# Distance lanes of a DTW kernel: one trip through memory in two parts, distances on unsplit fp32

## The chip, the cores and the metric

The kernel runs on one core of a Trainium2 chip. The metric is the device time of one execution, in microseconds (us). The engines are TensorE (PE), VectorE (DVE), ScalarE (ACT), GpSimd (POOL) and SyncE (SP, which only issues DMAs here).

## The reference

Two blocks, each a cross attention with a gate and a feed forward with a gate. The change touches only the "attention" of the first block, which is dynamic time warping of the 77 context rows against the 512 normalised tokens of each of 4 batches:

```
D = sqrt(max(aa + bb - 2 a @ b.T, 0))          # a: ctx 77x128, b: layernorm(x) 512x128
R[i,j] = D[i,j] + min(R[i-1,j], R[i,j-1], R[i-1,j-1])
path  = backtrack R from (76, 511) to (0, 0)   # first of diagonal, up, left that is smallest
x     = x + tanh(g_xattn[0]) * (sum over path of ctx[i] into row j)
x     = x + tanh(g_ffn[0])   * MoE(layernorm(x), 64 experts of 64, top 8, a shared expert)
x     = x + tanh(g_xattn[1]) * attention(layernorm(x), ctx, 16 heads)
x     = x + tanh(g_ffn[1])   * MoE(layernorm(x), 8 experts of 344, top 2, a shared expert)
```

## The kernel before

Each engine has one instruction stream, written out by hand; semaphores join them, and nothing reorders. The stages before the first feed forward are these.

**Norm.** `norm(0)` goes over the four batches b. DVE takes statistics and normalises three of four 128x128 tiles (`normalise`, L1244), GpSimd the fourth (L601). TensorE transposes them into a PSUM bank (`turn`, L951). ScalarE copies the bank to `xn_hi` in fp32r (`high`, L741) and squares it into `sq` (L744), and DVE forms the rest, `xn_lo` (`low`, L1253). `context` prepares the context: -2 times its transpose split into `ctxT_hi` (ACT, L728) and `ctxT_lo` (DVE, L1326), and its squared sums `aa` (L1329).

**Distances.** `distances(b)` on TensorE adds four products into a bank: hi by hi (L967), lo by hi (L968), ones by `sq` (L970, fp32) and hi by `xn_lo` (L972). ScalarE then does, for one batch after another, Relu with bias `aa` (L776), Sqrt (L778) and Square of the root (L780). The root is corrected in `corrected(b)` on DVE: an integer estimate of 1/(2 root) (L1340), the error d2 - root^2 (GpSimd at L642 for batches 0 to 2, DVE at L1345 for batch 3), times the estimate (L1347), plus the root (L1349).

**Lanes.** The recurrence runs as a skewed wave: 16 lanes for each batch (partitions 32b to 32b+15), 32 columns for each lane, 92 slots in time. The corrected rows (77 partitions) must become lanes with a skew, and go through memory for it: SP stores `drows` of each batch into `scr_d`, which was zeroed from the cleared lane buffer `dl` (GpSimd memset, L583), with a destination step that gives the skew (L463, 154 KB in runs of 128 bytes), and loads it back as lanes (L467, 184 KB, 16 rows of 11.8 KB). All four stores are issued ahead of the first load. DVE, SP and GpSimd wait for all four loads.

**Wave and path.** DVE runs 92 slots of four or five small instructions (L1384 to L1388, L1376), then 92 slots back (L1423 to L1427). The path goes through memory in three parts (`store_path` L406, `load_path` L413), half of the batches on SP's queue, half on ACT's; TensorE multiplies it with the context (L1006), and `norm(1)` begins. Beside the wave, GpSimd, TensorE and ScalarE transpose the weights of the second feed forward (`prep_in`, L632, L995, L806).

Before the wave, DVE also clears the edges of the backward pass (L1356 to L1360) and splits the first two groups of weights (`first_lo(0)`, L1366); the latter lets SP load the next group (`raw0(2, 0)`).

Of the kernel before, what the change touches and what calls it, by code (L numbers as in the profile page):

```python
# [29 lines left out]
P = 128  # L30
# [5 lines left out]
def program(nc, x, ctx_1024, g_xattn, g_ffn, r0_w, sg0, su0, sd0, eg0, eu0, ed0,  # L36
# [12 lines left out]
    SLOTS = KEYS + CH - 1  # L49
    LANE = SLOTS * CW  # L50
# [48 lines left out]
    with ctx:  # L99
# [31 lines left out]
        gates = sb("gates", [P, 4])  # L131
        tgate = sb("tgate", [P, 4])
        ctx_sb = sb("ctx_sb", [KEYS, B, H])
        ctxT = sb("ctxT", [P, B, KEYS])
        ctxT_hi = sb("ctxT_hi", [P, B, KEYS], F32R)
        ctxT_lo = sb("ctxT_lo", [P, B, KEYS], F32R)
# [58 lines left out]
        drows = view([B, S])  # L195
# [138 lines left out]
        s_cthi = sem("ctxT_hi_ready")  # L334
        s_ctlo = sem("ctxT_lo_ready")
# [4 lines left out]
        s_err = sem("dist_root_error")  # L340
        s_dist = sem("dist_ready")
        s_dst = [sem(f"dist_stored{b}") for b in range(B)]
        s_dld = [sem(f"dist_lanes{b}") for b in range(B)]
# [22 lines left out]
        def wait_low(engine, k, b):  # L366

            pool_before = POOL_LOW * min(max(k - 1, 0), 2)
            if k in (1, 2) and b < POOL_LOW:
                engine.wait_ge(s_xlp, pool_before + b + 1)  # L370
            else:
                engine.wait_ge(s_xlo, B * k + b + 1 - pool_before - (POOL_LOW if k in (1, 2) else 0))
# [28 lines left out]

        def store_path(engine, part, b):
# [14 lines left out]
        POOL_CONST = 10 + B  # L417
# [3 lines left out]
        def _(sp):  # L421
# [34 lines left out]
            sp.wait_ge(s_pool, POOL_CONST)  # L456
# [3 lines left out]
            for b in range(B):  # L460

                sp.wait_ge(s_dist, b + 1)
                sp.dma_start(at(scr_d[b], 0, [[CW, KEYS], [LANE + CW, CH], [1, CW]]),  # L463
                             drows[0:KEYS, b, :].rearrange("i (c w) -> i c w", w=CW)).then_inc(s_dst[b], 16)
            for b in range(B):
                sp.wait_ge(s_dst[b], 16)
                sp.dma_start(dl[LANES[b]:LANES[b] + CH].rearrange("c s w -> c (s w)"),  # L467
                             scr_d[b].rearrange("c s w -> c (s w)")).then_inc(s_dld[b], 16)

            for b in range(B):  # L470
                sp.wait_ge(s_dld[b], 16)
# [9 lines left out]
            sp.wait_ge(FF[0]["wlo"], 1)  # L481
            raw0(2, 0)
            for part in range(len(ON_PARTS)):
                for b in range(B // 2):
                    store_path(sp, part, b)
                for b in range(B // 2):
                    load_path(sp, part, b)

# [78 lines left out]
        def _(pool):  # L567
# [15 lines left out]
            nc.gpsimd.memset(dl, 0.0).then_inc(s_pool, 1)  # L583
            nc.gpsimd.memset(rst[:, 0, :], BIG).then_inc(s_pool, 1)
            pool.wait_ge(s_pool, 10)
# [37 lines left out]
            for g in range(GROUPS[1]):  # L623
# [14 lines left out]
                if g == 1:  # L638
                    for b in range(B - 1):

                        pool.wait_ge(s_root, b + 1)
                        nc.gpsimd.tensor_tensor(d2[0:KEYS, b, :], d2[0:KEYS, b, :], droot2[0:KEYS, b, :],  # L642
                                                ALU.subtract).then_inc(s_err, 1)
                    attention_prep()
                    for b in range(B):
                        pool.wait_ge(s_dld[b], 16)
# [77 lines left out]
        def _(act):  # L724
            def context():
                act.wait_ge(s_ct, 1)
                nc.scalar.activation(ctxT[:], ps[6][:, 0:B * KEYS].rearrange("p (b k) -> p b k", b=B), ACT.Copy)
                nc.scalar.activation(ctxT_hi[:], ps[6][:, 0:B * KEYS].rearrange("p (b k) -> p b k", b=B),  # L728
                                     ACT.Copy, scale=-2.0).then_inc(s_cthi, 1)
# [7 lines left out]
            def high(k, b):  # L737
                act.wait_ge(s_xt, B * k + b + 1)
                bank = turn_bank(k, b)
                if k == 0:  # L740
                    nc.scalar.activation(xn_hi[:, sl(b)], bank[:], ACT.Copy).then_inc(s_xhi, 1)  # L741
# [3 lines left out]
                else:  # L745
# [3 lines left out]
                    nc.scalar.activation(xn_hi[:, sl(b)], bank[:], ACT.Copy).then_inc(s_xhi, 1)  # L749

# [6 lines left out]
            def norm(k):  # L757
                for b in range(B):
# [5 lines left out]
                    if k == 2 and b >= 2:  # L764
                        query(b - 2)
                if k in (0, 2):
# [4 lines left out]

            norm(0)
            act.wait_ge(s_aa, 1)
            for b in range(B):
                act.wait_ge(s_ab, b + 1)
                nc.scalar.activation(d2[0:KEYS, b, :], dist_bank(b), ACT.Relu, bias=aa[:, b:b + 1]).then_inc(s_d2, 1)  # L776
                act.wait_ge(s_d2, b + 1)
# [934 lines left out]
```

## Time and profile before

| | us |
|---|---|
| median of three timed runs | 823.42 (819.32 to 824.99) |
| the profiled execution's own time | 818.27 |
| its span | 816.3 |
| busy in the span: TensorE, VectorE, ScalarE, GpSimd | 666.1, 624.9, 412.2, 412.8 |

The profiled execution is one run; about 2 us of its time lie around the span. The busy shares are averages over stages: from 44 to 160 us VectorE works alone through the wave, and from 200 us on TensorE is almost always busy.

### The profile page before, as it was taken

To read this page: it belongs to the slowest core of one execution; us is meant where nothing else is said; L and a number is where in the kernel's file an instruction comes from. 1 tells how busy PE (TensorE), PEld (TensorE's weight loads), DVE (VectorE), ACT (ScalarE), POOL (GpSimd) and SP (SyncE) were. 2 spreads that over 40 slices of the span, in tenths; PEclk is the share of its full clock that TensorE was granted. 3 is DMA by queue.
4 is the path that set the end of the run, shared out by engine and by line. 5 is a ranking of instruction groups with operands and counts; after the bars stand their busy time and mean duration, and the time that the engine had idled before them with its cause. 6 is when DMAs were issued, how large, how long until landed. Compare 5 with 4: busy or idle time off the path is not lost.

```text
span 816.3 us, 13236 instructions
## 1 busy us (share of the span) xinstructions
PE 666.1 (82%) x3082; PEld 535.1 (66%) x3082; DVE 624.9 (77%) x2076; ACT 412.2 (50%) x755; POOL 412.8 (51%) x448
## 2 busy tenths in 40 slices
PE   4412320089999999999999969999899999999995
PEld 2201110077787887888888748999878888888884
DVE  7689999877777777777777688777777777777774
ACT  3524410044566566656656555555556656665663
POOL 5367750026666666666666641110146666666663
PEclk9655555558999999999999969999789999999999
DMA  5545331104967676777767300000126666566761
GB/s 136 81 108 144 117 108 33 32 5 94 169 143 161 136 156 135 161 144 151 155 136 161 80 0 12 1 0 0 37 39 138 160 147 153 132 165 137 154 141 52
DMA packets 78728, 85.97 MB, mean 105 GB/s; under 512 B 44085, under 2 KB 56742, under 8 KB 75620
## 3 DMA queue, kind: packets, MB, share of 16 engines
q1 hardware_dynamic: 71638, 75.23, 43.6%
q0 software_dynamic: 4320, 9.68, 4.0%
q10 hardware_dynamic: 2734, 0.69, 0.4%
q8 instruction: 10, 0.16, 0.1%
q14 instruction: 26, 0.21, 0.1%
HBM read 76.69 MB, written 8.70 MB: 105 GB/s over the span
## 4 chain that ended last, share of the span: by engine, by line
PE 70%; DVE 20%; issue 4%; DMA 2%; ACT 2%; POOL 1%; DVEq 0%; ACTq 0%; POOLq 0%
PE bank L1012 14%; PE bank L1014 14%; PE bank L1013 14%; PE bank L1147 7%; PE bank L1145 6%; PE bank L1144 6%; PE bank L1074 4%; DVE arena L1427 3%; PE bank L1058 2%; DVE arena L1423 2%; DVE arena L1384 2%; DVE arena L1376 2%; DVE arena L1424 1%; DVE arena L1385 1%; PE bank L951 1%
## 5 line engine op out<-in xcount | busy, mean ns | idle before, releaser
L701 POOL TENSOR_TENSOR act_lo<-arena,act_hi 128x512 fp32r<-128x512 f32 x232 | 300.3, 1294 | 194.6 <-ACT act_hi L841 152.8
L1644 DVE TENSOR_TENSOR bank<-arena,bank 128x512 f32<-128x512 f32 x220 | 152.4, 693 | 102.9 <-ACT arena L855 71.8
L855 ACT ACTIVATE arena<-bank 128x512 f32<-128x512 f32 x232 | 139.2, 600 | 180.6 <-PE bank L1014 180.6
L1012 PE MATMUL bank<-xn_hi,w_hi 128*128 128x512 f32 x464 | 186.5, 402 | 1.2 <-DVE arena L1642 1.2
L1014 PE MATMUL bank<-xn_lo,w_hi 128*128 128x512 f32 x464 | 184.8, 398 | 0.0
L1013 PE MATMUL bank<-xn_hi,w_lo 128*128 128x512 f32 x464 | 184.2, 397 | 0.0
L1652 DVE TENSOR_TENSOR arena<-bank,arena 128x512 f32<-128x512 f32 x220 | 152.1, 691 | 13.8 <-DMA arena<-scr_mask 1.6
L841 ACT ACTIVATE act_hi<-arena 128x512 fp32r<-128x512 f32 x232 | 145.4, 627 | 9.3 <-DVE arena L1642 5.9
L1012 PEld LDWEIGHTS bank<-xn_hi,w_hi 128*128 128x128 f32 x464 | 88.4, 190 | 24.4 <-issue 2.0
L1014 PEld LDWEIGHTS bank<-xn_lo,w_hi 128*128 128x128 f32 x464 | 88.3, 190 | 21.9
L1013 PEld LDWEIGHTS bank<-xn_hi,w_lo 128*128 128x128 f32 x464 | 88.4, 190 | 21.0
L1147 PE MATMUL bank<-act_lo,w_hi 128*128 128x512 f32 x232 | 92.7, 399 | 3.3 <-POOL act_lo L701 3.3
L1145 PE MATMUL bank<-act_hi,w_lo 128*128 128x512 f32 x232 | 92.1, 397 | 0.0
L1144 PE MATMUL bank<-act_hi,w_hi 128*128 128x512 f32 x232 | 91.3, 393 | 0.0
L995 PE MATMUL bank<-ident,prep_in 128*128 128x128 f32 x75 | 22.5, 438 | 62.1 <-DMA prep_in<-in_L_ffn_wd 60.3
L601 POOL TENSOR_SCALAR xn<-x_res,mv,rstd 128x128 f32<-128x128 f32 x16 | 14.1, 883 | 96.7 <-DVE rstd L1301 72.6
L995 PEld LDWEIGHTS bank<-ident,prep_in 128*128 128x128 f32 x75 | 12.6, 213 | 72.0 <-DMA prep_in<-in_L_ffn_wd 70.2
L1147 PEld LDWEIGHTS bank<-act_lo,w_hi 128*128 128x128 f32 x232 | 43.6, 188 | 15.3 <-POOL act_lo L701 5.9
L1628 DVE TENSOR_TENSOR w_lo<-w_raw,w_hi 128x384 fp32r<-128x384 f32 x54 | 50.9, 943 | 0.8 <-ACT w_hi L849 0.8
L1144 PEld LDWEIGHTS bank<-act_hi,w_hi 128*128 128x128 f32 x232 | 43.6, 188 | 10.6 <-ACT act_hi L841 0.5
L1145 PEld LDWEIGHTS bank<-act_hi,w_lo 128*128 128x128 f32 x232 | 43.6, 188 | 10.1
L1006 PE MATMUL bank<-ctx_sb,arena 77*128 77x128 f32 x32 | 7.2, 425 | 47.4 <-DMA arena<-scr_on 47.4
(188 smaller groups left out, 949.2 us busy)
## 6 DMA issues: line engine op xcount, KB each, us to landing
arena<-scr_mask SPq DMA_DIRECT2D x94, 512.0 KB, 6.6
scr_w<-prep_out POOLq DMA_DIRECT2D x25, 192.0 KB, 2.2
w_raw<-scr_w SPq DMA_DIRECT2D x25, 192.0 KB, 6.3
w_raw<-in_L_ffn_expert_gate_k SPq DMA_DIRECT2D x32, 64.0 KB, 6.0
w_raw<-in_L_ffn_expert_up_k SPq DMA_DIRECT2D x32, 64.0 KB, 5.7
w_raw<-in_L_ffn_expert_down_k SPq DMA_DIRECT2D x64, 32.0 KB, 5.3
prep_in<-in_L_ffn_wg POOLq DMA_DIRECT2D x21, 64.0 KB, 2.4
prep_in<-in_L_ffn_wu POOLq DMA_DIRECT2D x21, 64.0 KB, 2.1
```

The source lines that it names most:

```text
L701: nc.gpsimd.tensor_tensor(act_lo[:, k % 2, :], act_a[:, k % 2, :], act_hi[:, k % 2, :].bitcast(F32), ALU.subtract).then_inc(FF[f]["alo"], 1)
L841: nc.scalar.activation(act_hi[:, j, :], act_a[:, j, :], ACT.Copy).then_inc(FF[f]["ahi"], 1)
L855: nc.scalar.activation(act_s[:, k % 2, :], ps[4 + k % 2][:], ACT.Silu).then_inc(FF[f]["silu"], 1)
L1012: nc.tensor.matmul(out, w_h, x_h, start=start, stop=False)
L1013: nc.tensor.matmul(out, w_l, x_h, start=False, stop=False)
L1014: return nc.tensor.matmul(out, w_h, x_l, start=False, stop=stop)
L1144: nc.tensor.matmul(ps[n][:], w_hi[:, j, DOWN:DOWN + P], act_hi[:, i, :], start=first, stop=False)
L1145: nc.tensor.matmul(ps[n][:], w_lo[:, j, DOWN:DOWN + P], act_hi[:, i, :], start=False, stop=False)
L1147: nc.tensor.matmul(ps[n][:], w_hi[:, j, DOWN:DOWN + P], act_lo[:, i, :], start=False, stop=last).then_inc(FF[f]["down"], 1)
L1628: nc.vector.tensor_tensor(w_lo[:, j, :], w_raw[:, j, :], w_hi[:, j, :].bitcast(F32), ALU.subtract).then_inc(FF[f]["wlo"], 1)
L1644: nc.vector.tensor_tensor(ps[6 + i][:], act_s[:, i, :], ps[6 + i][:], ALU.mult).then_inc(FF[f]["t"], 1)
L1652: nc.vector.tensor_tensor(act_a[:, i, :], ps[6 + i][:], mask[:, j, 512 * k:512 * (k + 1)], ALU.mult).then_inc(FF[f]["act"], 1)
```

## The change

1. The distances are formed on fp32 operands as they are: `xT0` (ScalarE's copy of the transposed tokens) times `ctxT_neg`, plus ones by `sq`. `ctxT_lo`, `xn_lo` of norm 0 and their waits are gone. `xT0` takes the place of `drows` in the arena, and `corrected` writes its result into `d2`.
2. DVE forms the root's error for all four batches; GpSimd's three instructions are gone.
3. ScalarE clears `dl` at the very start (L583's memset is gone from GpSimd), after a Sqrt of one column that has the table loaded; it does `dist_root(0)` ahead of `high(0, 3)`.
4. Each batch is stored in two parts (rows 0 to 23 and 24 to 76), and loaded in two (slots 0 to 23 and 24 to 91). The first part's loads are issued among the stores. DVE waits for the first parts ahead of slot 0 and for the second ahead of slot 24. SP and GpSimd wait for the first parts only.
5. The edges of the backward pass are cleared inside the wave (slots 16 to 21), and `first_lo(0)` follows the last path cells; SP's `raw0(2, 0)` follows the path's DMAs.

```diff
+    LSPLIT = 24
+    DIST_PARTS = [(0, LSPLIT), (LSPLIT, KEYS)]
+    LANE_PARTS = [(0, LSPLIT), (LSPLIT, SLOTS)]
...
+        def store_dist(engine, part, b):
+            first, last = DIST_PARTS[part]
+            engine.dma_start(at(scr_d[b], first * CW, [[CW, last - first], [LANE + CW, CH], [1, CW]]),
+                             d2[first:last, b, :].rearrange("i (c w) -> i c w", w=CW)).then_inc(s_dst[part][b], 16)
+        def load_lanes(engine, part, b):
+            first, last = LANE_PARTS[part]
+            for p in range(part + 1):
+                engine.wait_ge(s_dst[p][b], 16)
+            engine.dma_start(dl[LANES[b]:LANES[b] + CH, first:last].rearrange("c s w -> c (s w)"),
+                             scr_d[b, :, first:last].rearrange("c s w -> c (s w)")).then_inc(s_dld[part][b], 16)
+        def lanes_laid(engine, part):
+            for b in range(B):
+                engine.wait_ge(s_dld[part][b], 16)
...
             for b in range(B):
                 sp.wait_ge(s_dist, b + 1)
-                sp.dma_start(at(scr_d[b], 0, ...), drows[0:KEYS, b, :]...).then_inc(s_dst[b], 16)
+                store_dist(sp, 0, b)
+                store_dist(sp, 1, b)
+                if b >= 1:
+                    load_lanes(sp, 0, b - 1)
+            load_lanes(sp, 0, B - 1)
             for b in range(B):
-                sp.wait_ge(s_dst[b], 16)
-                sp.dma_start(dl[LANES[b]:LANES[b] + CH]..., scr_d[b]...).then_inc(s_dld[b], 16)
-            for b in range(B):
-                sp.wait_ge(s_dld[b], 16)
+                load_lanes(sp, 1, b)
+            lanes_laid(sp, 0)
...
-            nc.gpsimd.memset(dl, 0.0).then_inc(s_pool, 1)
...
+            nc.scalar.activation(root_one[:], ones[:, 0:1], ACT.Sqrt)
+            nc.scalar.activation(dl, ones[:, 0:CW].unsqueeze(1).broadcast_to([P, SLOTS, CW]), ACT.Copy, scale=0.0).then_inc(s_blank, 1)
             norm(0)
-            for b in range(B):
+            for b in range(1, B):
+                dist_root(b)
...
+                if k == 0:
+                    act.wait_ge(s_aa, 1)
+                    dist_root(0)
                 if k in (0, 2):
                     high(k, B - 1)
...
-                nc.tensor.matmul(d, ctxT_hi[:, b, :], xn_hi[:, sl(b)], start=True, stop=False)
-                nc.tensor.matmul(d, ctxT_lo[:, b, :], xn_hi[:, sl(b)], start=False, stop=False)
+                nc.tensor.matmul(dist_bank(b), ctxT_neg[:, b, :], xT0[:, b, :], start=True, stop=False)
                 pe.wait_ge(s_sq, b + 1)
-                nc.tensor.matmul(d, ones[:, 0:KEYS], sq[:, b % 2, :], start=False, stop=False)
-                pe.wait_ge(s_xlo, b + 1)
-                nc.tensor.matmul(d, ctxT_hi[:, b, :], xn_lo[:, sl(b)], start=False, stop=True).then_inc(s_ab, 1)
+                nc.tensor.matmul(dist_bank(b), ones[:, 0:KEYS], sq[:, b % 2, :], start=False, stop=True).then_inc(s_ab, 1)
...
-                if b < B - 1:
-                    dve.wait_ge(s_err, b + 1)
-                else:
-                    inv = done(nc.vector.tensor_tensor(d2[0:KEYS, b, :], d2[0:KEYS, b, :], droot2[0:KEYS, b, :], ALU.subtract))
+                inv = done(nc.vector.tensor_tensor(d2[0:KEYS, b, :], d2[0:KEYS, b, :], droot2[0:KEYS, b, :], ALU.subtract))
...
-            first_lo(0)
-            for b in range(B):
-                dve.wait_ge(s_dld[b], 16)
...
+                if s in (0, LSPLIT):
+                    lanes_laid(dve, 0 if s == 0 else 1)
...
+                if CH <= s < CH + 2 + B:
+                    back_edge(s - CH)
...
             cells(SLOTS // PIECE - 1)
+            first_lo(0)
```

Three places in the instruction streams show it. The names in brackets are semaphores: `dist_ready` counts corrected batches, `dist_stored` and `dist_lanes` the landings of stores and loads.

ScalarE, end of the norm and first roots, before:

```order
L741 ACTIVATE xn_hi<-bank 128x512 [waits xn_transposed]
L744 ACTIVATE arena<-bank 128x512 [waits dist_products]
L741 ACTIVATE xn_hi<-bank 128x512 [waits xn_transposed]
L744 ACTIVATE arena<-bank 128x512 [waits dist_products]
L776 ACTIVATE arena<-bank,aa 77x512 [waits dist_products,ctx_squared_sums]
L778 ACTIVATE arena<-arena 77x512 [waits dist_squared]
L780 ACTIVATE arena<-arena 77x512 [waits act_step]
```

and the same place after the change:

```order
L753 ACTIVATE arena<-bank 128x512 [waits xn_transposed]
L756 ACTIVATE arena<-bank 128x512 [waits dist_products]
L766 ACTIVATE arena<-bank,aa 77x512 [waits dist_products,ctx_squared_sums]
L768 ACTIVATE arena<-arena 77x512 [waits dist_squared]
L770 ACTIVATE arena<-arena 77x512 [waits act_step]
L753 ACTIVATE arena<-bank 128x512 [waits xn_transposed]
L756 ACTIVATE arena<-bank 128x512 [waits dist_products]
```

The three steps of `dist_root(0)` now stand ahead of the copy and the square of batch 3.

SP's queue, from the zeroing of the scratch to the first copy of the values, before:

```order
L457 DMA scr_d<-arena 64x2944 [waits pool_step]
L463 DMA scr_d<-arena 77x16x32 [waits dist_ready,scratch_zeroed]
L463 DMA scr_d<-arena 77x16x32 [waits dist_ready] x3
L467 DMA arena<-scr_d 16x2944 [waits dist_stored0]
L467 DMA arena<-scr_d 16x2944 [waits dist_stored1]
L467 DMA arena<-scr_d 16x2944 [waits dist_stored2]
L467 DMA arena<-scr_d 16x2944 [waits dist_stored3]
L478 DMA v_flat<-v_ext 77x4x9 [waits dist_lanes3,dist_lanes2,v_ready,dist_lanes1,dist_lanes0]
```

and after the change, from batch 2 on:

```order
L407 DMA scr_d<-arena 24x16x32 [waits dist_ready]
L407 DMA scr_d<-arena 53x16x32
L415 DMA arena<-scr_d 16x768 [waits dist_stored0_1]
L407 DMA scr_d<-arena 24x16x32 [waits dist_ready]
L407 DMA scr_d<-arena 53x16x32
L415 DMA arena<-scr_d 16x768 [waits dist_stored0_2]
L415 DMA arena<-scr_d 16x768 [waits dist_stored0_3]
L415 DMA arena<-scr_d 16x2176 [waits dist_stored1_0,dist_stored0_0]
L415 DMA arena<-scr_d 16x2176 [waits dist_stored1_1,dist_stored0_1]
L415 DMA arena<-scr_d 16x2176 [waits dist_stored1_2,dist_stored0_2]
L415 DMA arena<-scr_d 16x2176 [waits dist_stored1_3,dist_stored0_3]
L497 DMA v_flat<-v_ext 77x4x9 [waits dist_lanes0_3,dist_lanes0_2,v_ready,dist_lanes0_1,dist_lanes0_0]
```

The load of each first part stands behind the next batch's stores, and the large loads stand behind all of them.

VectorE, from the last batch's correction to the wave's first slot, before:

```order
L1340 TENSOR_SCALAR arena<-arena 77x512 [waits dist_root]
L1345 TENSOR_TENSOR arena<-arena 77x512
L1347 TENSOR_TENSOR arena<-arena 77x512 [waits dve_step]
L1349 TENSOR_TENSOR arena<-arena 77x512 [waits dve_step]
L1356 MEMSET arena 128x32 [waits dist_ready,pool_step]
L1357 MEMSET arena 128x33
L1360 MEMSET arena 16x33 [waits dve_step]
L1360 MEMSET arena 16x33 x3
L1366 TENSOR_TENSOR w_lo<-w_raw,w_hi 128x384 [waits ff0_whi,dve_step]
L1366 TENSOR_TENSOR w_lo<-w_raw,w_hi 128x384 [waits ff0_whi]
L1384 STREAM_SHUFFLE arena<-arena 128x1 [waits dist_lanes2,dist_lanes3,dist_lanes1,dist_lanes0]
```

and after the change:

```order
L1349 TENSOR_SCALAR arena<-arena 77x512 [waits dist_root]
L1351 TENSOR_TENSOR arena<-arena 77x512
L1353 TENSOR_TENSOR arena<-arena 77x512 [waits dve_step]
L1355 TENSOR_TENSOR arena<-arena 77x512 [waits dve_step]
L1392 STREAM_SHUFFLE arena<-arena 128x1 [waits dist_lanes0_2,dist_lanes0_1,dist_lanes0_3,dist_lanes0_0,pool_step]
```

Nothing stands between the correction and the wave any more; each of the four batches now has the four instructions that only batch 3 had.

## Rows read from the trace of the kernel before

**Rows 1.** Chain that ended last, first 200 us: start us, us, what.

```profile
16.77 0.57 PE bank L951 x4
...
34.53 3.00 DMA scr_d<-arena
37.55 6.10 DMA arena<-scr_d
...
162.19 2.62 DMA arena<-scr_on
```

**Rows 2.** Timeline of VectorE: start us, us, engine, line, operation; idle before in brackets.

```profile
43.78 0.01 DVE L1384 LOAD_MASK_SELECT arena<-arena  x1 [7.34 <-DMA arena<-scr_d]
...
46.26 0.15 DVE L1384 STREAM_SHUFFLE arena<-arena 128x1 f32<-128x1 f32 x1
```

**Rows 3.** Timeline of the start: GpSimd's clearing, and VectorE.

```profile
3.64 2.55 POOL L583 MEMSET arena<- 128x2944 f32 x1
...
6.62 0.18 DVE L1279 RECIPROCAL rstd<-std 128x4 f32<-128x4 f32 x1 [0.35 <-ACT std L735]
```

**Rows 4.** Loads of x issued from 1.7 to 2.2 us (one, at 1.84).

```profile
DMA to landing us min/median/max: 4.6/4.6/4.6
```

**Rows 5.** ScalarE's instructions by line and form: busy us, mean ns.

```profile
L890 ACT ACTIVATE arena<-arena 128x1232 f32<-128x1232 f32 x16 | 19.7, 1232 | 9.8 <-DVE arena L1539 9.8
```

**Rows 6.** Chain, first 22 us: TensorE's products of batch 0 and of batch 1.

```profile
12.43 1.35 PE bank L951 x4
...
14.63 1.71 PE bank L970 x2
...
17.33 0.23 PE bank L967
...
17.79 0.86 PE bank L970 x2
```

**Rows 7.** Timeline of ScalarE: end of the norm, first roots, last context step.

```profile
19.36 0.60 ACT L741 ACTIVATE xn_hi<-bank 128x512 fp32r<-128x512 f32 x1 [0.90 <-PE bank L951]
...
20.33 0.68 ACT L776 ACTIVATE arena<-bank,aa 77x512 f32<-77x512 f32 x1
...
22.24 0.67 ACT L776 ACTIVATE arena<-bank,aa 77x512 f32<-77x512 f32 x1
...
30.04 0.51 ACT L789 ACTIVATE kT_hi<-bank,bias 128x308 fp32r<-128x308 f32 x1
```

**Rows 8.** Timeline of VectorE and GpSimd while the roots are corrected.

```profile
22.44 1.52 DVE L1340 TENSOR_SCALAR arena<-arena 77x512 int32<-77x512 int32 x1 [1.27 <-ACT arena L780]
...
29.28 0.42 DVE L1340 TENSOR_SCALAR arena<-arena 77x512 int32<-77x512 int32 x1
...
29.80 0.69 DVE L1347 TENSOR_TENSOR arena<-arena 77x512 f32<-77x512 f32 x1
...
30.52 0.69 DVE L1349 TENSOR_TENSOR arena<-arena 77x512 f32<-77x512 f32 x1
30.63 0.89 POOL L594 TENSOR_TENSOR wq_lo<-w,wq_hi 128x128 fp32r<-128x128 f32 x1 [3.07 <-ACT kT_hi L789]
...
31.49 1.03 POOL L595 TENSOR_TENSOR kT_lo<-kT,kT_hi 128x308 fp32r<-128x308 f32 x1
...
31.73 1.33 DVE L1345 TENSOR_TENSOR arena<-arena 77x512 f32<-77x512 f32 x1
```

**Rows 9.** Issue to landing of the first lane load, at 34.86 us.

```profile
DMA to landing us min/median/max: 4.5/4.5/4.5
```

**Rows 10.** Issue to landing of the path's last stores (24 KB each, from 160.68 us).

```profile
DMA to landing us min/median/max: 1.5/1.6/1.7
```

**Rows 11.** Timeline of VectorE after the correction.

```profile
34.84 0.53 DVE L1360 MEMSET arena<- 16x33 f32 x4
35.41 1.03 DVE L1366 TENSOR_TENSOR w_lo<-w_raw,w_hi 128x384 fp32r<-128x384 f32 x2
```

**Rows 12.** Windows: busy us of PE, PEld, DVE, ACT, POOL; granted clock; DMA share; GB/s.

```profile
580.00:600.00 20.00, 18.50 (x72) 16.01 (x72) 16.50 (x95) 9.77 (x19) 3.88 (x4) 0.57 0.15 37
```

More of the change, by code:

```diff
@@ L339, in program @@
         s_root = sem("dist_root")
-        s_err = sem("dist_root_error")
         s_dist = sem("dist_ready")
-        s_dst = [sem(f"dist_stored{b}") for b in range(B)]
-        s_dld = [sem(f"dist_lanes{b}") for b in range(B)]
+        s_blank = sem("lanes_blank")
+        s_dst = [[sem(f"dist_stored{part}_{b}") for b in range(B)] for part in range(2)]
+        s_dld = [[sem(f"dist_lanes{part}_{b}") for b in range(B)] for part in range(2)]
         s_upper = sem("wave_upper")
@@ L371, in wait_low @@
             else:
-                engine.wait_ge(s_xlo, B * k + b + 1 - pool_before - (POOL_LOW if k in (1, 2) else 0))
+                engine.wait_ge(s_xlo, B * (k - 1) + b + 1 - pool_before - (POOL_LOW if k in (1, 2) else 0))
         def query_bank(n):
@@ L487, in _ @@
                     load_path(sp, part, b)
+            sp.wait_ge(FF[0]["wlo"], 1)
+            raw0(2, 0)
             def mask0(g, j, chunks, loaded):
@@ L638, in _ @@
                 if g == 1:
[L639 to L643, printed above, removed]
                     attention_prep()
-                    for b in range(B):
-                        pool.wait_ge(s_dld[b], 16)
+                    lanes_laid(pool, 0)
                 if g >= 1:
@@ L1309, in norm @@
                         context()
-                    if k == 0 and p >= 1:
-                        low(k, p - 1)
                     if k in (1, 2) and p > POOL_LOW:
@@ L1315, in norm @@
                         query(p - 2)
-                low(k, B - 1)
+                if k > 0:
+                    low(k, B - 1)
                 if k == 2:
@@ L1367, in first_lo, with back_edge @@
                                             ALU.subtract).then_inc(FF[f]["wlo"], 1)
-            first_lo(0)
-            for b in range(B):
-                dve.wait_ge(s_dld[b], 16)
+            def back_edge(step):
+                if step == 0:
+                    done(nc.vector.memset(lg[:, SLOTS, :, :], 0.0))
+                if step == 1:
+                    done(nc.vector.memset(qex[:, SLOTS, :], 0.0))
+                    settle()
+                if step >= 2:
+                    b = step - 2
+                    done(nc.vector.memset(qex[LANES[b]:LANES[b] + CH, SLOTS, :], 1.0))
             shift = [31] + list(range(CH - 1)) + [31] * (32 - CH)
```

68 lines of the change are left out of this document (24 added, 44 removed).

## The prediction

> **What bounds the kernel now.** I read the chain that ended last first. Up to 200 us it is one thread: norm, TensorE's products, ScalarE's roots, VectorE's correction, then two DMAs in a row, then the wave. The two DMAs are 3.00 us of store and 6.10 us of load, of batch 3 [rows 1], and the timeline of VectorE shows the same from its side: it sits idle for 7.34 us until the last lanes land, and the wave starts at 43.78 [rows 2]. So what counts is when the wave starts and whether the wave, the path and the feed forwards behind it keep their length. Nothing else in the first 44 us is worth anything by itself. The sum is made against the profiled execution's 818.27 us.
>
> **Before the distances.** GpSimd's clearing of `dl` takes 2.55 us and ends at 6.19; VectorE's next stage begins at 6.62 [rows 3]. It also needs batch 1 of x, which lands at 1.84 + 4.6 = 6.44 [rows 4], so freeing GpSimd gives 0.15 us at most here. ScalarE's clearing is 2944 columns; a form of 1232 columns takes 1.23 us [rows 5], so I put it at some 2.9 us, behind a table load that it has anyway. It ends near 5.2, when ScalarE's first work of the norm isn't ready. Cost 0. Dropping `ctxT_lo` takes some 0.25 us off VectorE, `xn_lo` of batch 0 another 0.6; so TensorE's second set of transposes, at 12.43 now [rows 6], starts at 12.0 and ends at 13.4.
>
> **TensorE.** Of the four products, ones by `sq` is fp32 and takes 1.71 us for batch 0 and 0.86 us for batch 1; an fp32r product takes 0.23 us at that later rate [rows 6]. The engine runs at half rate until about 16.7 us and at full rate after it. The new pair is twice fp32: 1.72 us in place of 0.86 + 3 x 0.23 = 1.55 at the full rate, and 3.4 in place of 3.0 at the half rate. Batch 0 is therefore done at 13.4 + 3.4 = 16.8, a little less if the rate rises as early as it starts work, and the transposes of batch 2 start where they start now, at 16.77 [rows 1]. The earlier start is spent on the longer product: gain 0.
>
> **ScalarE.** The transposes of batch 2 are done at 17.35. One copy and square take 20.33 - 19.36 = 0.97 us [rows 7], so `dist_root(0)` can start at 18.4, its product being done at 16.8. From there to VectorE's start is 22.44 - 20.33 = 2.11 us [rows 7, 8]: 20.5 in place of 22.44. The next batches of roots follow 1.91 us apart [rows 7], but batch 3's copy and square stand in between: `dist_root(1)` starts at 18.4 + 1.91 + 0.97 = 21.3, and roots 1, 2, 3 are there for VectorE at 23.4, 25.3 and 27.2.
>
> **VectorE's correction.** In peace L1340 takes 0.42, and two products in a row start 0.72 apart [rows 8]. One batch is then 0.4 + 0.72 + 0.72 + 0.61 = 2.45 us. Batch 0 runs 20.5 to 22.9, batch 1 23.4 to 25.9, batch 2 to 28.3, batch 3 to 30.8. Now it ends at 34.53 [rows 1], since GpSimd's share costs more than it takes off: L1340 took 1.52 us beside GpSimd's subtraction in place of 0.42, and L1345 1.33 beside `kT_lo` [rows 8]. One such meeting stays. ScalarE's last context step ends at 30.55, which is 4.5 us behind the start of `dist_root(3)` (20.33 + 3 x 1.91 = 26.06) [rows 7]; after the change that is 25.1 + 4.5 = 29.6, in the middle of batch 3, and `wq_lo` (0.89) and `kT_lo` (1.03) [rows 8] follow it. Bounds 0 and 1.9 us; I take 0.5, since VectorE's L1349 was not held up by `wq_lo` and its turn came between the two. Done at 31.3: **3.2 us earlier** (bounds 1.7 and 3.7).
>
> The Trainium skill (SBUF — State Buffer, "Who interferes with whom") says that a VectorE instruction with two SBUF inputs contends with a GpSimd one that reads SBUF, and that the first to issue keeps the other out for its whole length. The rows agree (L1345 31.73 to 33.06, GpSimd until 32.52) [rows 8]. By it the loss is that of whoever comes first, 0.5 or 1.5 us, within my bounds.
>
> **The two DMAs.** Before, 34.53 to 43.78: 9.25 us. The load's 6.10 are not its own: the first of the four loads took 4.5 us [rows 9], and the last one queued behind three. A part of 24 rows is 48 KB. For its store the nearest rows are 1.5 to 1.7 us (24 KB, long runs) [rows 10] and 3.00 (154 KB in runs of 128 bytes) [rows 1]; I take 2.1, since a third of the runs lies nearer to the small one. For its load, 3 KB a row, they are 2.62 for the path's last loads [rows 1], four at once on two queues, and 4.5 for rows of 11.8 KB [rows 9]; alone it should be less than 2.62, and I take 2.1, with 1.6 as the low end. With 0.1 for the semaphores that makes 4.3: **4.95 us less** (bounds 2.8 and 5.9). The loads of batches 0 to 2 are hidden in the correction; batch 3's second store, issued 0.3 us after the first, is moving its data while the first part's load is still being prepared.
>
> Here a rule speaks against the change. The Trainium skill (DMA: Bandwidth & Descriptors, "Anatomy of one DMA") puts a DMA at about 2.0 us plus its bytes over 436 GB/s, so that halves cost almost what the whole does. For the new pair it gives 4.2 us, like my sum; for the old pair it would give 4.8, where the rows have 9.1 [rows 1]. Here the measurement decides. By the rule's difference alone, 0.6 us in place of 4.95, the sum at the end would be 3.2 us.
>
> The wave starts at 31.3 + 4.3 = **35.6 in place of 43.78**, 8.2 us earlier.
>
> **The wave and behind it.** A slot is 0.61 us (four from 43.81 to 46.26) [rows 2]; slot 24 comes 14.7 us after the start, at 50.3. The four second loads are issued by about 35.5, and four larger ones landed 9 us after the first was issued (34.86 to 43.78); even with the values' copies and GpSimd's weights on the same queues they have 5 us in hand: cost 0. The six clearings of the edge move from a wait into the wave. Four took 0.53 us [rows 11], so six are 0.8 in full; a slot has gaps of 0.16, so 0.25 is the low end; I take **0.6 added**. `first_lo(0)`, 1.03 us [rows 11], moves to where VectorE waits for the path's last trip, until beyond 164.8 from 160.7 [rows 1]; cost 0, or 1 if its cover were gone. It releases `raw0(2, 0)`, four issues on SP that stand behind the path's loads and whose group is used some 40 us later. GpSimd's preparation of weights waits for first parts now and moves with the wave.
>
> **Sum.** 3.2 + 4.95 = 8.2 (rounded) less 0.6 = **7.6 us**: 818.27 becomes 810.7. The profiled execution lies 5.15 us below the median of the timed runs, 823.42, so I forecast 823.4 - 7.6 = **815.8**. The bounds of the terms give 1.7 + 2.8 - 0.8 = 3.7 to 3.7 + 5.9 - 0.25 = 9.4, or 814.0 to 819.7.
>
> **Rivals.**
> 1. TensorE stays at the half rate through all distances. For: it has the rate of batch 0 [rows 6], and more work. Against: it rose at 16.7 us with the engine at work since 12.43, and after the change the engine works at least as densely, without the wait for `xn_lo`. Each batch then takes 3.4 + 1.35 us, the last product ends at 29.8, the correction 2.1 + 2.5 later at 34.4; the gain is 0.1 + 4.95 - 0.6 = 4.5: 818.9.
> 2. The legs don't shrink with the size. If the part's load takes the 4.5 us of [rows 9] and its store 3.0 [rows 1], the two give 9.25 - 7.6 = 1.65 and the sum is 4.3: 819.1. The rule of the Trainium skill named above (DMA: Bandwidth & Descriptors) says the same more strongly; with its difference alone one would be at 820.2.
> 3. The other side: the granted clock. Between 580 and 600 us it averaged 0.57 [rows 12], a stretch at 1.2 GHz that covers most of the window while TensorE is 92% busy, and no cause in the kernel is visible. Were such a stretch longer after the shift, each microsecond of full-rate work in it would cost one more; from 7.6 us of work on the change is a loss, and with 20 us it would be 12 us slower: 828. Against it: the work behind the wave is the same, in the same order.
> 4. The change does more than I take: the store and load at their low ends and no meeting with GpSimd, a gain of 9.4: 814.0.
>
> **How the numbers follow.** About 1% (8.2 us) is what a measurement of this kernel can tell from no change, since its own runs differ by 0.7%. The forecast's case (gain 5.5 to 8.6) gets 0.55, rival 4 0.2, rival 1 0.06, rival 2 0.12, rival 3 0.04, the rest 0.03. The timed runs before scatter by -4 and +1.6 us round their median. With that, 0.35 of the forecast's case and 0.9 of rival 4 end beyond 1%, and a fifth of rivals 1 and 2: 0.19 + 0.18 + 0.04, and 0.01 of the rest, is 0.42 for faster by over 1%. Slower by over 1% is rival 3 and 0.01 of the rest, 0.05; within 1% is what is left, 0.53. The range runs from 823.4 - 9.4 and the runs' scatter, 809, to rival 2 and a little scatter, 821.
>
> **What would show it.** The wave's first slot at 35.6 (34.4 to 40); the idle time ahead of it near 4.3 us; the first correction starting at 20.5 and the last one done at 31.3; the loads of first parts landing in some 2.1 us; no wait at slot 24; the wave's span longer by 0.6; the path's last trip and the feed forwards unchanged. It would be wrong if batch 3's first part landed late behind other traffic, if the wave were slowed by GpSimd's earlier work, or if a stretch of low clock moved.

## The result, and the profile after

| | before | changed |
|---|---|---|
| median of timed runs, us | 821.37 (818.05 to 824.99, 4 runs) | 846.03 (844.62 to 847.24, 4 runs) |
| ratio | | 1.0294 [1.0261, 1.0327] |
| span of the profiled execution, us | 816.3 | 844.5 |

The change costs 24.7 us; the prediction had it gain 7.6. The range (809 to 821) doesn't hold the result, and the rival on the slower side isn't what happened either.

The chain that ended last, of the changed kernel, answers to [rows 1] (columns: start, us, what):

```profile
16.22 0.45 PE bank L972 x4
...
29.11 0.85 DVE arena L1355
29.95 2.16 SPq L407
32.16 0.36 SPq L407
32.56 9.88 SPq L415
42.48 0.38 SPq L407
42.90 0.32 SPq L407
43.27 9.57 SPq L415
52.88 0.38 SPq L407
53.31 0.32 SPq L407
53.67 9.49 SPq L415
63.20 2.84 DMA arena<-scr_d
...
183.91 1.49 DMA scr_on<-arena
185.41 2.33 DMA arena<-scr_on
```

Up to 29.95 the thread is the old one, and it is early: before, the last correction ended at 34.53. Then comes what the chain of before doesn't have at all: 33 us of `SPq`, the issuing of DMAs on SP. Three issues of a load of a first part (L415) last 9.5 to 9.9 us each, where two stores in a row (L407) take 0.7. The timeline of VectorE shows the other side, against [rows 2]:

```profile
66.17 0.01 DVE L1392 LOAD_MASK_SELECT arena<-arena  x1 [36.23 <-DMA arena<-scr_d]
```

The idle time ahead of the wave grew from 7.34 us to 36.23, and the wave starts at 66.17 in place of 43.78, 22.4 us later.

What the DMAs do in that time is in the DMA view of 22 to 60 us (40 slices of 0.95 us: busy tenths of the 16 DMA engines, and GB/s), and in a window (us, busy time of PE, PEld, DVE, ACT, POOL, then granted clock, DMA share, GB/s):

```profile
DMA  0300111111140111111111510111111116111111
GB/s 0 55 14 13 11 11 11 11 11 11 11 58 11 11 11 11 11 11 11 11 11 11 99 21 11 11 11 11 11 11 11 11 11 106 15 11 11 11 11 11
```

```profile
34.00:41.00 7.00, 0.00 (x0) 0.00 (x0) 0.00 (x0) 0.00 (x0) 0.00 (x0) 0.50 0.10 11
```

The peaks are the first parts, 24 rows each. All the rest is a flat 11 GB/s: 106 KB of a second store at 11 GB/s are 9.6 us, which is the length of the long issues. A single store of 77 rows moved ten times as fast, as one more window of the kernel before shows (its first store, of batch 0, under way):

```profile
27.40:28.60 1.20, 1.20 (x5) 0.63 (x4) 1.10 (x2) 1.18 (x2) 0.16 (x1) 0.50 0.82 128
```

So the store of rows 24 to 76, in the same runs of 128 bytes, moves at a twelfth of the rate of the store of rows 0 to 76. The two differ in the number of rows: 77 = 7 x 11, and 53 is a prime. The Trainium skill (DMA: Bandwidth & Descriptors, "Why a DMA increments its semaphore by 16 and not by 1") says that a DMA runs on the largest number of engines up to 16 that divides the slowest dimension of both its sides, and on HWDGE (the way of DMAs that SP issues) on the lowest-numbered ones. By it 77 rows run on 11 engines, 24 on 12, and 53 on one. The measured rates agree with it: 128/11 = 11.6 GB/s for each engine, and 11 for one. So does a count in the traces. There the last packets of a DMA are completions of 4 bytes, which raise its semaphore. The DMA view of 27.2 to 28.8 us of the kernel before holds one store of 77 rows, which is 77 x 16 = 1232 runs of 128 bytes and 11 packets more:

```profile
DMA packets 1243, 0.16 MB, mean 99 GB/s; under 512 B 1243, under 2 KB 1243, under 8 KB 1243
```

The updates of each store's semaphore give the same count, after one early update at the issue: 11 at 77 rows and at 22 and 55, 12 at 24, 10 at 20, 9 at 54, 3 at 57, and 1 at 53 and at 23. In all kernels here it is the largest divisor up to 16. Which engines they are the traces don't say. The experiments change the number of rows and look at what becomes of the time.

Of the rest, rows that answer to [rows 3, 7, 8]:

```profile
2.21 2.64 ACT L798 ACTIVATE arena<-ones 128x2944 f32<-128x2944 f32 x1
6.30 0.18 DVE L1292 RECIPROCAL rstd<-std 128x4 f32<-128x4 f32 x1 [0.85 <-DMA x_res<-in_x]
19.77 0.42 DVE L1349 TENSOR_SCALAR arena<-arena 77x512 int32<-77x512 int32 x1 [3.33 <-ACT arena L770]
22.57 0.42 DVE L1349 TENSOR_SCALAR arena<-arena 77x512 int32<-77x512 int32 x1 [0.33 <-ACT arena L770]
28.94 0.45 POOL L612 TENSOR_TENSOR wq_lo<-w,wq_hi 128x128 fp32r<-128x128 f32 x1 [9.18 <-ACT kT_hi L810]
29.11 0.84 DVE L1355 TENSOR_TENSOR arena<-arena 77x512 f32<-77x512 f32 x1
```

The estimate L1349 takes 0.42 us each time, where L1340 had taken 1.52 in its place. From the wave's start on little is new: from its start to the last path cell 117.74 us (66.17 to 183.91) against 116.90, and no wait at slot 24. From the last path cell to the end of the span this execution has 660.6 us and the profiled one of before 655.6. That isn't the change: the profiled executions of e1 to e12 lie between 657.4 and 662.6, e6's, which has before's code behind the wave, at 660.0. Before's is the short one, beside e10's. The granted clock there is low in stretches, as in [rows 12]; here in three windows of the changed kernel:

```profile
600.00:610.00 10.00, 8.88 (x42) 8.44 (x41) 5.01 (x21) 3.26 (x10) 1.74 (x2) 0.50 0.00 0
610.00:620.00 10.00, 9.31 (x44) 8.62 (x43) 7.26 (x28) 4.92 (x9) 1.73 (x2) 0.50 0.32 75
620.00:630.00 10.00, 9.35 (x31) 6.50 (x32) 9.43 (x65) 4.95 (x8) 2.60 (x2) 0.84 0.00 0
```

The stretch at 1.2 GHz is longer here: 23.9 us by the clock's own records, against 17.1 in the profiled execution of before. The experiments have 23.9 or 27.4, but for e10's 17.1, so the short stretch goes with the short executions and not with the kernel before as such. What sets its length no run shows. With the two terms of the wave, 22.4 + 0.84 = 23.2 us stand beside the 24.7 of the medians.

### The profile page after: what moved, and what is told of

Same layout as the page of the kernel before. It is cut to its first block, busy times and chain, and to the rows that moved or that the text cites. A ratio compares the mean times of both kernels' runs of the same rounds, so it can differ in the third digit from the quotient of the medians.

```text
span 844.5 us, 13234 instructions
## 1 busy us (share of the span) xinstructions
PE 671.7 (80%) x3078; PEld 537.6 (64%) x3078; DVE 619.4 (73%) x2074; ACT 415.1 (49%) x757; POOL 406.7 (48%) x444
## 4 chain that ended last, share of the span: by engine, by line
PE 69%; DVE 18%; SPq 4%; issue 3%; ACT 2%; DMA 1%; POOL 1%; DVEq 0%; ACTq 0%; POOLq 0%
PE bank L1029 14%; PE bank L1031 14%; PE bank L1030 14%; PE bank L1164 6%; PE bank L1161 6%; PE bank L1162 6%; PE bank L1091 4%; SPq L415 3%; DVE arena L1438 3%; PE bank L1075 2%; DVE arena L1434 2%; DVE arena L1392 2%; DVE arena L1382 1%; DVE arena L1435 1%; DVE arena L1393 1%
## 5 line engine op out<-in xcount | busy, mean ns | idle before, releaser
L1029 PEld LDWEIGHTS bank<-xn_hi,w_hi 128*128 128x128 f32 x464 | 88.1, 190 | 24.7 <-DVE arena L1654 2.2
L827 ACT ACTIVATE prep_out<-bank 128x384 f32<-128x384 f32 x25 | 12.3, 490 | 82.1 <-PE bank L1012 82.1
```

Of the source, the lines that this page charges most:

```text
L1029: nc.tensor.matmul(out, w_h, x_h, start=start, stop=False)
```

## Experiments

Each is one edit of the changed kernel unless it says otherwise. Where the timed kernel has a ratio, it is to the kernel before, run beside it. Theory A is the number of rows; theory B the order and number of the DMAs on SP's queue, whatever their rows, theory C that a second store of this size in short runs is too much ahead of the loads, whatever its rows. Theory D, in e5 and e6, is about the rest of the change: in e5 that it costs time as well, in e6 that it gains none.

**e1: 22 and 55 rows**

```diff
-    LSPLIT = 24
+    LSPLIT = 22
```

> The changed kernel with the parts cut at row and slot 22 instead of 24, so the stores have 22 and 55 rows. Theory A (a store is spread over as many DMA engines as the largest number up to 16 that divides its row count; 53 is prime, so the second store ran on one engine at 11 GB/s, 9.5 us each, and held SP's queue): 22 and 55 both divide by 11, as 77 does, so the stores take some 1.2 us of data each, SP's issues are short, the wave starts at 34 to 35 instead of 66.15, and the kernel takes 812 to 816. Theory B (stores and loads alternating on one queue, or 16 DMAs instead of 8, hold SP's queue): nothing changes, 846. Theory C (the second store's 106 KB in runs of 128 bytes is simply too much ahead of the loads): with 55 rows it is a little worse, 847.

Measured: 815.35 (811.56 to 815.87), ratio 0.9901 [0.9865, 0.9938]. Two rows fewer in the first part take 30.7 us away. The chain, and the timeline of SP and VectorE:

```profile
30.73 1.67 DMA scr_d<-arena
32.42 1.91 DMA arena<-scr_d
```

```profile
26.61 0.56 SPq L415 DMA_DIRECT2D arena<-scr_d  x1
28.20 0.74 SPq L407 DMA_DIRECT2D scr_d<-arena  x2
28.98 0.54 SPq L415 DMA_DIRECT2D arena<-scr_d  x1
...
34.46 0.01 DVE L1392 LOAD_MASK_SELECT arena<-arena  x1 [3.76 <-DMA arena<-scr_d]
```

The load's issue is 0.55 us and the wave starts at 34.46. A window of 24 to 25 us has the stores' rate:

```profile
24.00:25.00 1.00, 0.00 (x0) 0.00 (x0) 0.96 (x2) 0.97 (x2) 0.00 (x0) 1.00 0.70 106
```

Same two parts, same order, same queue: the order and the split as such are not the cause.

**e2: 24 rows and 53, but the 53 as 48 and 5**

```diff
+            for r0, r1 in ([(first, last)] if part == 0 else [(first, first + 48), (first + 48, last)]):
```

> The changed kernel with the second store of each batch issued as two, of 48 and 5 rows; same bytes, one DMA more for each batch. Theory A: 48 rows go on 16 engines and 5 rows on 5, so the wave starts at about 35 and the time is some 813 to 817. Theory B: one more DMA in the same queue, at least as slow as the change, 846 or more. Theory C: as slow, 846.

One run: 814.81 (before beside it 823.11). The wave starts at 33.13:

```profile
33.13 0.01 DVE L1393 LOAD_MASK_SELECT arena<-arena  x1 [3.87 <-DMA arena<-scr_d]
```

The cut is that of the changed kernel and there is one DMA more in each batch, so neither the cut at 24 nor the number of DMAs costs anything. What was slow was the one DMA of 53 rows.

**e3: 23 and 54 rows**

```diff
-    LSPLIT = 24
+    LSPLIT = 23
```

> The changed kernel cut at 23, so the stores have 23 and 54 rows. Theory A: 23 is prime, so the first store, 47 KB, runs on one engine: 4.1 us of data, while the 54 rows go on 9 engines. The wave waits for the first part, so it starts about 3 us later than with 22 and 55: 37 to 39, and 816 to 820; SP's issues of the next DMA are held for up to 4 us. Theory B and C: as the change, 846, since one row more or less makes no difference.

One run: 827.03 (before beside it 823.11). Now the first part is the prime one. Windows of 23 to 26 us, and of 27.5 to 28 with a store of 54 rows:

```profile
23.00:26.00 3.00, 0.28 (x1) 0.30 (x2) 2.79 (x6) 2.91 (x6) 0.00 (x0) 1.00 0.07 10
```

```profile
27.50:28.00 0.50, 0.50 (x4) 0.33 (x2) 0.50 (x2) 0.50 (x1) 0.00 (x0) 0.50 0.72 107
```

10 GB/s for 23 rows and 107 for 54: the slow part moves with the prime. The place was right and the size was not, in the time (816 to 820 expected) as in the wave, which started at 46.85 and not at 37 to 39. I had counted batch 3's store alone, and four slow stores queued. The last one in the chain, from issue to landing:

```profile
38.64 6.27 DMA scr_d<-arena
```

**e4: the kernel before, its store cut into 24 and 53 rows, nothing else**

```diff
-                sp.dma_start(at(scr_d[b], 0, [[CW, KEYS], ...]), drows[0:KEYS, b, :]...).then_inc(s_dst[b], 16)
+                for r0, r1 in ((0, 24), (24, KEYS)):
+                    sp.dma_start(at(scr_d[b], r0 * CW, [[CW, r1 - r0], ...]), drows[r0:r1, b, :]...).then_inc(s_dst[b], 16)
```

> The kernel before with nothing changed but the store: each batch's 77 rows are stored as 24 and 53, all ahead of the loads, which stay whole. Theory A: the four stores of 53 rows take 9.5 us each on one engine, one after another from 27 us on, so the last lands near 66, the loads after it near 71, and the wave starts some 26 us late: 845 to 850. Theory B (alternation): no load stands among the stores, so nothing happens, 820 to 824.

One run: 853.62 (before beside it 823.11). The chain:

```profile
36.39 9.89 SPq L464
...
46.73 9.88 SPq L464
...
56.65 12.57 DMA scr_d<-arena
69.23 5.59 DMA arena<-scr_d
```

The cut alone, in a kernel with none of the change's other parts, makes the wave 31 us late (74.95). I expected 26 us and 845 to 850; the direction is that of theory A, the size 5 us more. Here no load and no wait on a store stands between the stores, and SP's issues still last 9.9 us: it is the issue that is held while the store right ahead of it moves, not a wait on a semaphore. It ends about 2 us before that store lands (46.29 and 48.30 for batch 1's). What holds it isn't shown by any run.

**e5: the changed kernel without the cut** (one store of 77 rows and one load for each batch, all stores ahead of the loads)

```diff
-    DIST_PARTS = [(0, LSPLIT), (LSPLIT, KEYS)]
-    LANE_PARTS = [(0, LSPLIT), (LSPLIT, SLOTS)]
+    DIST_PARTS = [(0, KEYS)]
+    LANE_PARTS = [(0, SLOTS)]
```

> The changed kernel without its split: one store of 77 rows and one load of 92 slots for each batch, all stores ahead of all loads, as before; unsplit fp32 distances, the correction on VectorE alone, ScalarE's clearing, the early first root and the moved clearings stay. In the changed kernel's own trace the correction ended at 29.95 instead of 34.53. Theory A (the loss is the 53 rows alone): the legs are those of before, 9.2 us, the wave starts at 39.2 to 40, 4 us earlier, less 0.9 us for the clearings in the wave: some 3 us faster than before, 818 to 821. Theory D (the unsplit distances and the correction cost time as well, hidden in the changed kernel behind the stores): no faster than before, 823 or more.

819.99 (816.89 to 821.64, 12 runs), ratio 0.9979 [0.9964, 0.9994]. The correction ends at 30.30, the DMAs are the old ones, and the wave starts at 39.60, 4.2 us earlier than before:

```profile
30.30 3.00 DMA scr_d<-arena
33.32 6.16 DMA arena<-scr_d
```

Less 0.9 for a longer wave, 3.3 us should be left, and the ratio shows 1.7 [0.5 to 3.0]. The missing part is no more than the scatter of what lies behind the wave (657.4 to 662.6 above), and wasn't followed. So the rest of the change gains a little and costs nothing, against theory D.

**e6: the kernel before with the cut alone, at 22** (`store_dist`, `load_lanes`, `lanes_laid` as in the change, `LSPLIT = 22`, nothing else)

> The kernel before with the split alone, cut at 22 (stores of 22 and 55 rows, first loads among the stores, VectorE waits at slots 0 and 22). In e1 the first part's legs took 1.67 and 1.91 us. Theory A: correction done at 34.53 as before, wave starts at 38.3 instead of 43.78: some 5.5 us faster, 816 to 819. Theory D: the whole gain of e1 (8 us) comes from the split: 814 to 816.

817.29 (812.11 to 818.98), ratio 0.9938 [0.9914, 0.9963]. Chain, and the start of the wave:

```profile
33.90 1.71 DMA scr_d<-arena
35.63 1.87 DMA arena<-scr_d
```

```profile
37.62 0.01 DVE L1403 LOAD_MASK_SELECT arena<-arena  x1 [1.82 <-DMA arena<-scr_d]
```

The cut brings 6.2 us of start by itself, the rest of the change 4.2 (e5), both together 9.3 (e1). The two don't add up because 0.6 of e6's is a correction that ended at 33.90 in this execution in place of 34.53, and e1's ended at 30.73, not at e5's 30.30. The legs alone are 5.5 us shorter in both.

**e10: 20 and 57 rows** (57 = 3 x 19)

```diff
-    LSPLIT = 24
+    LSPLIT = 20
```

> The changed kernel cut at 20, so the stores have 20 and 57 rows. The largest divisor of 57 up to 16 is 3. Theory A: the second store runs on 3 engines at 34 GB/s, 3.4 us each; they follow each other through the correction, the last first part is queued behind them on those engines, and the wave starts at 37.5 to 39, 3 to 4.5 us later than with 22 and 55: 817 to 821. If only prime row counts were bad, it would be 815 as e1; if any odd count that isn't a multiple of 11 were, 840 and more.

One run: 816.82 (before beside it 825.08); the wave starts at 39.94, a little beyond the 37.5 to 39 expected. The timeline of SP:

```profile
25.70 3.48 SPq L415 DMA_DIRECT2D arena<-scr_d  x1
...
29.99 3.16 SPq L415 DMA_DIRECT2D arena<-scr_d  x1
```

57 rows are 114 KB, in 3.5 us 33 GB/s, three times the rate of 53, and the held issue is a third as long. That is a step between the two cases, and speaks for the divisor and against an effect of primes alone. It is told by the rate, by the three completions and by the wave, 5.5 us behind e1's, and not by the total: 816.82 is only 1.5 above e1, since what lies behind the path was short in this one execution (657.4 against 661.7).

**e9: 24 and 53 rows, all first stores and first loads ahead of the second stores**

```diff
                 store_dist(sp, 0, b)
-                store_dist(sp, 1, b)
...
             load_lanes(sp, 0, B - 1)
+            for b in range(B):
+                store_dist(sp, 1, b)
```

The clearings of the edge moved with it to slots 24 to 29.

> The changed kernel, cut at 24 as it is, with SP's queue in another order: all four stores of 24 rows and all four first loads, and only then the four stores of 53 rows and the second loads; the backward edge is cleared at slots 24 to 29. Theory A: one engine still needs 4 x 9.5 us for the stores of 53 rows, from about 32 us on, so the second parts land near 72 to 74. The wave starts at about 34.5, its slot 24 comes at 49, and there VectorE waits some 23 to 25 us: 836 to 842, the stall moved from slot 0 to slot 24 and little smaller. Theory B (it is the alternation of stores and loads that holds the queue): no wait at slot 24, 815.

One run: 853.09 (before beside it 825.08). The chain, and VectorE at slot 24:

```profile
32.87 10.54 SPq L407
43.45 11.13 SPq L407
54.62 27.20 DMA scr_d<-arena
81.88 5.25 DMA arena<-scr_d
```

```profile
87.36 0.01 DVE L1393 LOAD_MASK_SELECT arena<-arena  x1 [38.36 <-DMA arena<-scr_d]
```

The order can't save it: the wave starts early (34.23) and stands still for 38 us at slot 24. I expected 23 to 25 there, and 836 to 842 in all. Four stores took 49 us (32.55 to 81.82), some 12 each and not 9.6, with GpSimd's weights moving beside them. That these take time from the one engine is an inference here, from the Trainium skill's "lowest-numbered" ones named above. For other DMAs the completions bear it out. In the changed kernel the load behind the 53-row store of batch 1 has 15 of its 16 completions by 43.94, and the last at 44.64, after that store's own at 44.41. Behind the 57-row store of batch 1 in e10 it is three that are late (13 by 30.64, the others 31.32 to 31.35, the store's own up to 31.13).

**e7: 22 and 55 rows, the edge cleared before the wave** (behind batch 3's stores, which read the same part of the arena)

```diff
+            back_edge(0)
+            for part in range(2):
+                dve.wait_ge(s_dst[part][B - 1], 16)
+            for step in range(1, B + 2):
+                back_edge(step)
+            settle()
...
-                if CH <= s < CH + 2 + B:
-                    back_edge(s - CH)
```

> e1 with the six clearings of the backward edge moved out of the wave to the wait for the first lanes, behind a wait for batch 3's stores, whose source they overwrite. The wave of the changed kernel was 0.86 us longer than that of before (117.76 against 116.90 us from first slot to last path cell). If the clearings in the wave are the reason, the wave takes 116.9 again and the kernel is 0.9 us faster than e1, the stores having landed before the lanes; if the wave waits for the clearings, nothing is gained.

815.12 (811.75 to 817.08), ratio 0.992 [0.9894, 0.9946]. From the wave's start to the last path cell it has 116.86 us against 117.69 in e1: the six clearings cost 0.83 us inside the wave. In the medians the two kernels can't be told apart.

**e8: e7 with the cut at 13**, so that stores have 13 and 64 rows

```diff
-    LSPLIT = 22
+    LSPLIT = 13
```

> As e7, but cut at 13: stores of 13 rows (13 engines) and 64 rows (16 engines), first loads of 13 slots (1.7 KB a row). Theory A: the first part's legs take some 1.5 and 1.6 us instead of 1.67 and 1.91, so the wave starts 0.4 us earlier than in e7; slot 13 comes 8 us after the start, when the second parts have landed. If they haven't, VectorE waits at slot 13 and the kernel is slower than e7.

812.88 (810.38 to 815.32), ratio 0.9894 [0.987, 0.9918]: the lowest median of all, 33 us under the changed kernel, though its interval overlaps those of e1 and e7. VectorE ahead of the wave:

```profile
32.69 0.09 DVE L1372 MEMSET arena<- 128x33 f32 x1 [3.20 <-DMA scr_d<-arena]
```

What ends the wait, as in e7 already (2.91 us there), is not a load but batch 3's second store, which the edge's clearing has to wait for. The wave starts at 33.41, 0.6 us before e7's, but not for the reason expected: the legs took 1.67 and 1.86 us, no less than e7's 1.70 and 1.82, and the correction had ended 0.85 us earlier in this execution (29.47 against 30.32). So neither the profile nor the medians show a gain of 13 over 22.

**e11: e7 with GpSimd's three subtractions back**

```diff
-                inv = done(nc.vector.tensor_tensor(d2..., d2..., droot2..., ALU.subtract))
+                if b < B - 1:
+                    dve.wait_ge(s_err, b + 1)
+                else:
+                    inv = done(nc.vector.tensor_tensor(d2..., d2..., droot2..., ALU.subtract))
```

> e7 with one part of the change undone: GpSimd forms the root's error for batches 0 to 2 again. In e7 the correction of four batches took 10.5 us from the first instruction to the last's end; in the kernel before it took 12.1. Theory A2 (GpSimd's share costs VectorE more than it takes off, since the two keep each other from the port): the correction ends 1 to 2 us later, the wave starts that much later than in e7's trace (counted from the first L1349). Rival (VectorE is bound by ScalarE's roots, 1.9 us apart, and GpSimd's share hides): no difference above 0.3 us.

815.69 (811.71 to 817.94), ratio 0.9916 [0.9892, 0.994]. VectorE and GpSimd in batch 0:

```profile
18.92 2.00 DVE L1355 TENSOR_SCALAR arena<-arena 77x512 int32<-77x512 int32 x1 [2.91 <-ACT arena L776]
```

```profile
19.32 1.31 POOL L661 TENSOR_TENSOR arena<-arena 77x512 f32<-77x512 f32 x1
```

The estimate takes 2.00 us beside GpSimd's subtraction and 0.42 without it. From first start to last end the correction has 12.3 us (18.92 to 31.2) against 10.1 (20.13 to 30.25; the 10.5 of the expectation is too high): 2.2 us. This profiled run had its first root 1.2 us earlier, so the wave is only 1.0 later (34.97), and the medians don't separate.

**e12: e7 with ScalarE's `high(0, 3)` ahead of `dist_root(0)` again**

```diff
+                if k in (0, 2):
+                    high(k, B - 1)
                 if k == 0:
                     act.wait_ge(s_aa, 1)
                     dist_root(0)
-                if k in (0, 2):
-                    high(k, B - 1)
```

> e7 with another part undone: ScalarE takes the copy and square of batch 3 ahead of the first root again. The first correction starts 1 us later, but the second was held by ScalarE for 0.3 us in e7 already, so the end of the correction moves by 0.6 to 0.7 us only. Rival: the whole 1 us, or nothing if VectorE is bound by the last root.

816.26 (812.06 to 817.62), ratio 0.9935 [0.9903, 0.9966]. The first correction starts at 22.01 in place of 20.13, the last ends and the wave starts 1.5 us later (35.50). I expected 0.6 to 0.7: the root now waits for TensorE's transposes of batch 3 as well as for the copy, 1.9 us and not 1.0.

## Why the prediction was wrong

**The step that failed is "The two DMAs"**, in two places. The store of a part was priced by its bytes and the length of its runs (bounds 1.5 to 3.0 us, from [rows 10] and [rows 1]), and the second store was taken to be "moving its data while the first part's load is still being prepared", with no time of its own in the sum. Its data take some 9.6 us, since its 53 rows have no divisor up to 16 but one. And the price does not stay with it: SP is held in the very next issue until about 2 us before the slow store lands (42.44 and 44.41 for batch 1's), so three of the four second stores stand in full ahead of batch 3's first load (9.88 + 9.57 + 9.49 = 28.94 us in L415), and "the four second loads are issued by about 35.5" falls with it (63.72 to 65.16). That they cost nothing at slot 24 held, behind a wave that was late itself. e1, e2, e3 and e10 changed only where the rows are cut and gave 815.35, 814.81, 827.03 and 816.82 in place of 846.03; e4 put the loss into the kernel before by the cut alone. The prediction weighed one rule of the Trainium skill's page on DMAs, the fixed time, and not the one on the number of engines. And the fixed time is fitted there for DMAs that GpSimd issues, which the prediction doesn't say; these are SP's, and the new pair took 3.6 us in e1 where that rule gives 4.2. No row of before has a DMA with such a row count, and the bounds, drawn from the nearest in bytes, were near in the wrong respect.

Where the row count divides, the forecast's terms can be read in e1, whose median of 815.35 is 0.45 us from the forecast, 815.8. That it is so near is partly luck: in its profile the wave starts 1.1 us earlier than forecast, and the medians show only 0.2 of it, the rest going to the longer wave and to scatter.

| term | predicted | measured |
|---|---|---|
| first correction starts | 20.5 | 20.53 in e1; 20.13 (e7), 19.77 (changed) |
| last correction ends | 31.3, 3.2 earlier | 30.73 in e1, 3.8 earlier; 30.30 (e5), 29.95 (changed): 4.2 and 4.6 |
| store and load of batch 3's first part | 2.1 + 2.1, 4.95 less | 1.67 + 1.91 in e1; 9.10 - 3.58 = 5.5 less |
| wave starts | 35.6 | 34.46 in e1, 66.17 as changed |
| clearings inside the wave | 0.6 | 0.83 |
| ScalarE's clearing of `dl` | 2.9 | 2.64 |
| gain in the end | 7.6 | 7.8 in e1 (823.11 to 815.35) |

- **Before the distances** was right in kind. VectorE's stage begins at 6.30 in place of 6.62; the gain of 0.3 is more than the 0.15 allowed, since x landed earlier in this execution, and it still ends the wait.
- **TensorE**: taken as a gain of 0, and it was one in e1. The granted clock rose at 17.5 us there, both products of batch 0 took 1.7 us each as forecast, and ScalarE's first root started at 18.42. In the changed kernel's execution the clock rose at 15.7; there the transposes of batch 2 start at 16.22 and not 16.77, and 0.55 us came of it. Rival 1, half rate throughout, is out: it has the last correction end at 34.4, and it ended at 30.73 in e1.
- **ScalarE** was right. e12 shows `dist_root(0)` first to be worth 1.5 us of start, more than its own part of the sum.
- **VectorE's correction** was right in cause (e11: 2.2 us from GpSimd's subtraction) and small by 0.6 us at its end in e1, and by 1.4 in the changed kernel, where 0.7 of it is the earlier start; the meeting with `wq_lo`, taken at 0.5, cost 0.15 (L1355 took 0.84 us beside it, and 0.69 in peace).
- **The wave and behind it**: no wait at the cut's slot in any kernel with split loads but e9, the path's last load 2.33 us against 2.62, and the clearings as in the table.
- **Rival 2** (the legs keep their length) and **rival 4** (all terms at their good ends) are told by e6: the legs are 1.71 + 1.87 us, so rival 2 is out, and the forecast's case lies near rival 4 in the start of the wave. **Rival 3** predicted slower by way of the granted clock. It isn't what happened: the 22.4 us are lost ahead of the wave, with TensorE idle. Its price was off too: 20 us of work, 12 us slower than 823.4, would be 836 and not 828. Behind it the profiled execution has 5.0 us more than before's, but e1 has as many (661.7 from last cell to end), and is faster in the medians all the same.
- **The bounds** of the two DMAs, 2.8 and 5.9, don't come out of the rows named: 1.5 + 1.6 + 0.1 gives 6.05 less, and 2.8 leaves 6.45 us for two legs, for which no row is named. The measured 5.5 lies inside either way.

Left open: why the medians of e5 and of e7, e11 and e12 differ by less than the starts of their waves, and what in SP's queue holds an issue.

## What to carry to other kernels

Before a DMA is cut into parts, look at the number of rows of each part, not only at its bytes: the rate here went by the largest divisor up to 16 of the outer count, and 53 rows moved at 11 GB/s where 77 moved at 128. Choose the cut so that both parts divide well, or give the remainder a DMA of its own (48 + 5). And price a slow DMA twice, for its own length and for what its queue issues behind it, since the issue behind it was held here nearly as long as the transfer took.

## What the runs showed of the hardware

Rates of stores in runs of 128 bytes, by row count:

| rows | 77 | 54 | 22, 55 | 57 | 23 | 53 |
|---|---|---|---|---|---|---|
| GB/s | 128 | 107 | 106 | 33 | 10 | 11 |
| largest divisor up to 16 | 11 | 9 | 11 | 3 | 1 | 1 |

- That is some 10 to 12 GB/s for each unit of the divisor, and the completions of each store in the traces number the divisor.
- SP's issue right behind a slow store is held: 9.5 to 9.9 us at 53 rows in the changed kernel (up to 13.2 in e9), 3.1 to 3.5 at 57, while behind 55 rows it took 0.55. It ended 1.9 to 2.0 us before the slow store's landing in the changed kernel and at 57 rows. What holds it isn't shown.
- A DMA issued right behind a slow store has as many late completions as that store has completions: 1 at 53 rows, 3 at 57.
- A load of 16 rows of 2.8 KB took 1.9 us, one of 11.8 KB 4.5 as the first of four [rows 9] and 6.1 behind others. Row length and bytes grow together here, and no run separates them.
